# Moving three weight and operand splits at the end of a latent attention and in the routing of its mixture of experts

## The chip, the cores and the metric

The kernel runs on one core of a Trainium2 chip. The metric is the device time of the whole program in microseconds (us), as the median of several runs. The engines are named as in the profile: PE is TensorE (PEld its weight loads), DVE is VectorE, ACT is ScalarE, POOL is GpSimd and SP is SyncE, which issues the loads.

## The reference

One perceiver layer for 256 tokens of 512 features, in float32:

```python
x = x + xattn(layernorm(x), ctx)    # 1 head of 512, 4096 context rows + the 256 tokens
x = x + mla(layernorm(x))           # 16 heads, query rank 192, key/value rank 128, rotary part 64, causal
x = x + moe(layernorm(x))           # 32 routed experts of width 256, 8 a token out of 4 of 8 groups, and a shared expert
# mla: out = concat_h(softmax(q_h k_h^T * scale) v_h) @ Wo
# moe: sum_e weight_e * (silu(x Wg_e) * (x Wu_e)) @ Wd_e + shared(x)
```

The kernel computes every expert for every token and multiplies by the routing weight, which is zero for the experts not chosen. The shared expert is stored as experts 0 and 1 of 34, with weight 1.

## The kernel before

**Precision.** Each float32 operand is used as a pair: a high part, rounded by a cast, and a low part, the difference. A product is three matmuls, high by high, high by low and low by high (`product`, lines 411 to 415). So every weight and every intermediate result needs a cast on ACT (`split_hi`, line 277; `out_hi`, 305) and then a subtraction on DVE (`split_lo`, 282; `out_lo`, 309).

**Weights** come in tiles through a ring of two slots (`Tile`, `slot = s % 2`), each in two loads by SP (line 369), part a with piece 0 and part b with pieces 1 and 2. A load waits until the low part of the piece that was in its slot is made (`lo_split`). `split_hi` waits for its load and until PE has used the piece before (`used`); `split_lo` waits for `split_hi`; PE waits for `split_lo` (`ready`). A tile of the attention (`T_M + pair`) has piece 0, the projections of two heads (896 columns), and piece 1, their rows of the output weights Wo (1024). A tile of an expert (`T_E + e`) has piece 0 (gate weights and a quarter of up, 1280), piece 1 (down, 1024) and piece 2 (the rest of up, 768).

**Order.** Every engine's instructions are written out by hand and run in that order; the engines meet in counting semaphores. `ev_lo` counts the low parts of results that DVE has made, and PE waits for values of it.

**The latent attention** handles its 16 heads as 8 pairs. In `pair_step(j, s)` PE scores pair s, projects pair s + 1, transposes the softmax of pair s and multiplies the output of pair s - 1 by its rows of Wo. ACT and DVE handle the results; at the end of the step ACT makes the high parts of piece 0 of tile s + 3 and of Wo of pair s + 1, and DVE the low part of piece 0 of tile s + 3. The low part of Wo of pair s DVE makes at the beginning of step s. Steps 5 and 6, the last in the loop, split the first pieces of experts 0 and 1, which stand in the ring behind the attention. The low part of the last Wo tile (pair 7, `Tile(0, T_M + PAIRS - 1)`, piece 1) is made by POOL, behind its rotary work and ahead of two small roots for the norm.

**The tail** handles pair 7 on its own, by halves of the queries: PE runs `values_pair` of pair 6, `score_last`, then the Wo product of pair 6 behind the low part of its output (`pair_out_lo`). DVE masks the scores (`last_bias`), ACT exponentiates (`last_exp`), DVE normalizes, PE transposes (line 830), and so on to the residual, the third norm (`norm_stats`, `normalize`) and the transposed tokens (`xt_hi`, `xt_lo`). Then `expert_rows` runs experts 0 and 1 by half of the tokens, in the order (0, half 0), (1, half 0), with the second half's transposes in the middle, (0, half 1), (1, half 1).

**The experts.** PE alternates `gate_up` of one expert and `down` of the expert before: expert 2, down 1, expert 3, down 2, expert 4, down 3, and so on. DVE makes the hidden rows (`expert_product`, line 1555) and, after ACT's cast (line 1175), their low part (`expert_lo`, 1560), then the splits of later weights (`expert_splits(j, s)`: piece 1 of expert s + 1 and pieces 0 and 2 of expert s + 2 of the step), then adds the expert's rows to the residual (`expert_add`, 1548). The routing (lines 1574 to 1620, some 30 small DVE instructions) runs between expert 0's add and expert 1's. In it stand `expert_product(1, 0)` and `expert_lo(1, 0)`, which are of expert 2.

Of the kernel before, what the change touches and what calls it, by code (L numbers as in the profile page):

```python
# [45 lines left out]
PAIRS = HEADS // 2  # L46
# [12 lines left out]
T_WQ, T_WK, T_CT, T_WV, T_CN, T_WO, T_QKV, T_M = 0, 1, 2, 10, 11, 19, 20, 21  # L59
T_E = T_M + PAIRS  # L60
# [6 lines left out]
M_SIZES = (896, 1024)  # L67
E_SIZES = (1280, 1024, 768)
# [42 lines left out]
def perceiver_layer(nc, x, small, wq, wk, wv, wo, ctx_t, ctx_n, w_qkv, w_rope, w_mla, w_exp, out):  # L111
    with ExitStack() as ctx:
# [3 lines left out]
        def sem(name):  # L116
            return ctx.enter_context(nc.semaphore(name))
# [109 lines left out]
        lo_split = [sem(f"lo_split{k}") for k in range(3)]  # L227
# [44 lines left out]
        def split_hi(act, t, k, sizes, first=False):  # L272
            act.wait_ge((loaded_b if k else loaded_a)[t.slot], t.loaded)
            if not first:
                act.wait_ge(used[k], t.free(k))
            at, n = OFF[k], sizes[k]
            act.copy(w_hi[:, t.slot, at:at + n], raw[:, t.slot, at:at + n]).then_inc(hi_split[k], 1)  # L277

        def split_lo(eng, t, k, sizes):
            eng.wait_ge(hi_split[k], t.split(k))  # L280
            at, n = OFF[k], sizes[k]
            eng.tensor_tensor(w_lo[:, t.slot, at:at + n], raw[:, t.slot, at:at + n],  # L282
                              w_hi[:, t.slot, at:at + n].bitcast(F32), ALU.subtract) \
               .then_inc(lo_split[k], 1)
# [690 lines left out]
        def _(act):  # L975
# [97 lines left out]
            def pair_qk_hi(j, s, hd):  # L1073
                out_hi(act, 4 + 3 * hd, j * 2 + ((F7 if hd else F4)["qk"] + s), flat(mqk_hi[:, hd, :, :]), 512)
# [4 lines left out]
            def pair_out_hi(j, s):  # L1079
                out_hi(act, 5, j * 2 + (F5["o"] + s), flat(mo_hi[:, :, :]), 512)  # L1080

            def head_exps(j, s, hd):
                for i, (h, at, n) in enumerate(((1, 0, T), (0, T, P))):
                    act.wait_ge(m_bias_ready, j * 8 + (4 * s + 2 * hd + i + 1))
                    k = 2 * hd + h
                    p = pair_probs[:, hd, at:at + n]
                    act.activation(p, p, ACT.Exp, bias=m_bias[:, k:k + 1], scale=-1.0,
                                   accum_out=m_sum[:, k:k + 1]).then_inc(m_exp, 1)
# [4 lines left out]
            def pair_step(j, s, sizes=M_SIZES):  # L1093
                head_exps(j, s, 0)
                if not (isinstance(j, int) and s == 0):
                    pair_out_hi(j, s - 1)
                head_exps(j, s, 1)
                for hd in range(2):
                    pair_qk_hi(j, s + 1, hd)
                    head_probs_hi(j, s, hd)  # L1100
                pair_v_hi(j, s + 1)
                split_hi(act, Tile(j, T_M + s + 3), 0, sizes)
                split_hi(act, Tile(j, T_M + s + 1), 1, M_SIZES)

            for hd in range(2):
# [7 lines left out]
                pair_step(j, 1)  # L1113
                pair_step(j, 2)
            pair_step(0, PAIRS - 3, E_SIZES)
            pair_step(0, PAIRS - 2, E_SIZES)

            def last_exp(h, hd):
                act.wait_ge(m_bias_ready, 4 * (PAIRS - 1) + 2 * h + hd + 1)
# [6 lines left out]
            def last_probs_hi(h):  # L1126
                out_hi(act, 2 + h, F23["pt"] + 2 * (PAIRS - 1), last_pt_hi[h], 256 * (h + 1))
# [7 lines left out]
            last_exp(1, 1)  # L1135
            half_hi(act, 4, F4["o_last"], mo_hi, 0, 2)
            last_probs_hi(1)
            split_hi(act, Tile(0, T_E + 1), 2, E_SIZES, first=True)
            half_hi(act, 5, F5["o_last"], mo_hi, 1, 2)
            split_hi(act, Tile(0, T_E), 1, E_SIZES)  # L1140
# [48 lines left out]
        def _(dve):  # L1189
# [8 lines left out]
            def norm_stats(h, midway=None):  # L1198

                then(dve.bn_stats(stat[:, h, :], res[:, h, :]))  # L1200
                if midway is not None:
                    midway()
                then(dve.bn_aggr(mean_var[:, h, :], stat[:, h, :]))
                dve.tensor_scalar(var_eps[:, h:h + 1], mean_var[:, h, 1:2], LN_EPS, None, ALU.add) \
                   .then_inc(var_ready, 1)

            def normalize(h, roots):

                dve.wait_ge(rstd_ready, roots)
                dve.tensor_scalar(xn[:, h, :], res[:, h, :], mean_var[:, h, 0:1], rstd[:, h:h + 1],  # L1210
                                  ALU.subtract, ALU.mult).then_inc(xn_ready, 1)
# [222 lines left out]
            def pair_step(j, s, sizes=M_SIZES):  # L1434
                n = j * (2 * PER_PAIR) + (V_MLA + s * PER_PAIR - 1)
                for hd in range(2):
                    head_bias(j, s, hd)
                split_lo(dve, Tile(j, T_M + s), 1, M_SIZES)
                head_normalize(j, s, 0)
                if not (isinstance(j, int) and s == 0):  # L1440
                    pair_out_lo(n)
                head_normalize(j, s, 1)
                for hd in range(2):
                    head_qk_lo(n + 1 + 2 * hd, hd)
                    head_probs_lo(n + 2 + 2 * hd, hd)
                pair_v_lo(n + 5, s + 1)
                split_lo(dve, Tile(j, T_M + s + 3), 0, sizes)

            for hd in range(2):
                head_qk_lo(V_M0 + hd, hd)  # L1450
# [5 lines left out]
                split_lo(dve, Tile(0, T_M + k), 0, M_SIZES)  # L1456
            for i in range(PAIRS - 3):
                pair_step(0, i)
            for i in range(PAIRS - 3, PAIRS - 1):
                pair_step(0, i, sizes=E_SIZES)  # L1460


            def last_bias(h):
# [33 lines left out]
            add_to_residual(0, F01["y"], 1, 4)  # L1497
            tokens_lo(dve, 2, V_LN3, xt_hi, xt_lo, 0)
            norm_stats(1)
            normalize(1, 8)  # L1500
            split_lo(dve, Tile(0, T_E + 1), 2, E_SIZES)
            tokens_lo(dve, 0, V_LN3 + 2, xt_hi, xt_lo, 1)
            dve.wait_ge(lo_split[1], Tile(0, T_M + PAIRS - 1).split(1))
            split_lo(dve, Tile(0, T_E), 1, E_SIZES)


# [34 lines left out]
            def expert_add(j, s):  # L1541
                for h in range(2):
                    b = 4 + 2 * (s % 2) + h
                    first = {4: F4, 5: F5, 6: F6, 7: F7}[b]["moe"]
                    dve.wait_ge(bank_full[b], j + (first + s // 2))
                    dve.wait_ge(res_done, j * 4 + (3 + 2 * s + h))
                    w = weights[:, h, bass.ds(j * 2 + s, 1)]
                    dve.scalar_tensor_tensor(out=res[:, h, :], in0=bank[b][:, :], scalar=w, in1=res[:, h, :],  # L1548
                                             op0=ALU.mult, op1=ALU.add).then_inc(res_done, 1)
# [8 lines left out]
            def expert_lo(j, s):  # L1558
                dve.wait_ge(ev_hi, j * 2 + (V_H + s))
                dve.tensor_tensor(h_lo[:, s % 2, :], h_row[:, s % 2, :], h_hi[:, s % 2, :].bitcast(F32),  # L1560
                                  ALU.subtract).then_inc(ev_lo, 1)
# [35 lines left out]
            then(dve.tensor_tensor(cubed(ties), other, own, ALU.is_equal))  # L1597
            then(dve.tensor_tensor(ties, ties, smalls[:, C_TIE:C_TIE + 128], ALU.mult))
            then(dve.tensor_tensor(beats, beats, ties, ALU.add))
            expert_lo(1, 0)  # L1600
            then(dve.tensor_reduce(rank, beats.rearrange("p (g k) -> p g k", k=GROUPS), AX, ALU.add))
            then(dve.tensor_scalar(chosen_g, rank, float(TOP_GROUPS), None, ALU.is_lt))

# [17 lines left out]
            def expert_splits(j, s):  # L1621
                split_lo(dve, Tile(j, T_E + s + 1), 1, E_SIZES)
                for k in (0, 2):
                    split_lo(dve, Tile(j, T_E + s + 2), k, E_SIZES)
# [9 lines left out]
                                             in1=res[:, h, at:at + n], op0=ALU.mult, op1=ALU.add).then_inc(res_done, 1)  # L1634

            expert_add(0, 1)
            expert_splits(1, 0)
            expert_add(1, 0)
            expert_hidden(1, 1)
# [16 lines left out]
        @block.gpsimd  # L1656
        def _(pool):
            def root(n, at, cols):

                pool.wait_ge(var_ready, n)  # L1660
                pool.tensor_tensor(rstd[:, at:at + cols], var_eps[:, at:at + cols], power[:, at:at + cols],
                                   ALU.pow).then_inc(rstd_ready, 1)

            pool.memset(zero_r.bitcast(F32)[:, :], 0.0).then_inc(zeroed, 1)
            pool.memset(power[:, :], -0.5).then_inc(power_set, 1)
            pool.wait_ge(power_set, 1)
            for h in range(2):
                root(h + 1, h, 1)
            for n, at, cols in ((3, 0, 1), (4, 1, 1), (5, 2, 2), (6, 4, 2)):
                root(n, at, cols)  # L1670
            pool.wait_ge(q_raw_ready, 4)
            for pair in range(1, PAIRS):
                if pair == 1:
                    pool.wait_ge(bank_full[5], F5["rope_t"])
                else:
                    pool.wait_ge(bank_full[3], F23["pt"] + 2 * (pair - 2))
                turn_queries(pool, pair, 3 * pair)
            pool.wait_ge(lo_split[1], Tile(0, T_M + PAIRS - 1).split(1) - 1)
            split_lo(pool, Tile(0, T_M + PAIRS - 1), 1, M_SIZES)
            for h in range(2):  # L1680
                root(7 + h, h, 1)

# [88 lines left out]
```

## Time and profile before

| what | value |
|---|---|
| median of 3 runs | 547.72 us (545.03 to 547.96) |
| profiled execution | 546.07 us, of which the span of the instructions 544.3 us |
| mean granted clock of PE | 0.987 |
| busy PE, DVE, ACT, POOL | 97%, 72%, 55%, 5% of the span |
| DMA | 85.98 MB, 158 GB/s on the mean |
| chain that ended last | PE 89%, DVE 5%, DMA 2%, ACT 2% |

"Busy" is the share of the span in which an engine has an instruction under way. PE's clock is granted at one of two levels, 2.4 GHz (1.00 in the rows) and 1.2 GHz (0.50). The chain is followed back from the last instruction through whatever released each step. Times of rows are microseconds from the first instruction.

### The profile page before, as it was taken

The page shows a single profiled execution, that of the slowest core. Times are in us where ns is not written, and L with a number is a line of the kernel's source. Part 1 is how long each engine was busy: PE and PEld are TensorE (multiplying, and loading weights), DVE is VectorE, ACT ScalarE, POOL GpSimd, SP SyncE. Part 2 cuts the span into 40 slices and gives each one's busy share as a digit, 9 for nine tenths or more (in the row PEclk, how much of TensorE's full clock was granted, in tenths as well). Part 3 has the DMA queues.
Part 4 walks back from the last instruction along what each step waited for, and adds up shares of the span by engine and source line. Part 5 has one row for each costly group of instructions (what it writes and reads, how often), then busy time and mean ns, then how long its engine had stood idle before and what let it go on. Part 6 is the DMA issues. An engine that isn't in the chain of part 4 may idle for free.

```text
span 544.3 us, 9657 instructions
## 1 busy us (share of the span) xinstructions
PE 526.4 (97%) x3454; PEld 473.8 (87%) x3454; DVE 390.8 (72%) x621; ACT 302.0 (55%) x470; POOL 25.0 (5%) x43
## 2 busy tenths in 40 slices
PE   9999999999869999989989999999999999999998
PEld 7988888887659898869879999999999999999997
DVE  6776666557696888676777677776777767777675
ACT  4664597654355676654645646456464564645632
POOL 1000000000131213020000000000000000000000
PEclk9999999999996999989999999999999999999999
DMA  8766524555022224333526554646546465564521
GB/s 289 261 222 198 188 78 155 164 173 173 8 90 83 74 81 152 116 117 101 214 92 193 212 183 164 225 142 211 182 165 223 145 210 182 165 224 145 209 69 39
DMA packets 19459, 85.98 MB, mean 158 GB/s; under 512 B 2160, under 2 KB 2416, under 8 KB 19440
## 3 DMA queue, kind: packets, MB, share of 16 engines
q1 hardware_dynamic: 19440, 85.73, 46.9%
q8 instruction: 11, 0.18, 0.1%
q14 instruction: 8, 0.07, 0.0%
HBM read 85.20 MB, written 0.52 MB: 158 GB/s over the span
## 4 chain that ended last, share of the span: by engine, by line
PE 89%; DVE 5%; DMA 2%; ACT 2%; issue 1%; SPq 0%; POOL 0%; ACTq 0%; DVEq 0%; POOLq 0%
PE bank L411 27%; PE bank L415 27%; PE bank L414 27%; DMA raw<-w_exp_dram 2%; DVE w_lo L282 2%; PE bank L483 1%; PE bank L419 1%; PE bank L555 1%; PE bank L693 1%; PE bank L420 1%; PE bank L421 1%; DVE operands L309 1%; DVE scores L1403 1%; ACT w_hi L277 1%; PE bank L713 1%
## 5 line engine op out<-in xcount | busy, mean ns | idle before, releaser
L277 ACT CAST w_hi<-raw 128x768 fp32r<-128x768 f32 (+3 forms) x158 | 159.0, 1039 | 140.2 <-PE bank L411 124.3
L282 DVE TENSOR_TENSOR w_lo<-raw,w_hi 128x1024 fp32r<-128x1024 f32 (+3 forms) x157 | 184.3, 1215 | 15.5 <-ACT w_hi L277 13.4
L411 PE MATMUL bank<-xt_hi,w_hi 128*128 128x256 f32 x544 | 154.2, 283 | 2.8 <-DVE w_lo L282 2.7
L414 PE MATMUL bank<-xt_lo,w_hi 128*128 128x256 f32 x544 | 154.0, 283 | 0.0
L415 PE MATMUL bank<-xt_hi,w_lo 128*128 128x256 f32 x544 | 154.0, 283 | 0.0
L411 PE MATMUL bank<-w_hi,operands 128*128 128x512 f32 (+1 forms) x322 | 126.4, 393 | 2.5 <-DVE operands L309 1.6
L415 PE MATMUL bank<-w_hi,operands 128*128 128x512 f32 (+1 forms) x322 | 124.6, 387 | 0.0
L414 PE MATMUL bank<-w_lo,operands 128*128 128x512 f32 (+1 forms) x322 | 124.3, 386 | 0.0
L411 PEld LDWEIGHTS bank<-xt_hi,w_hi 128*128 128x128 f32 x544 | 103.5, 190 | 4.9 <-DVE w_lo L282 3.1
L414 PEld LDWEIGHTS bank<-xt_lo,w_hi 128*128 128x128 f32 x544 | 103.5, 190 | 1.2
L415 PEld LDWEIGHTS bank<-xt_hi,w_lo 128*128 128x128 f32 x544 | 103.5, 190 | 0.0
L411 PEld LDWEIGHTS bank<-w_hi,operands 128*128 128x128 f32 x322 | 60.8, 189 | 13.1 <-DVE operands L309 1.9
L415 PEld LDWEIGHTS bank<-w_hi,operands 128*128 128x128 f32 x322 | 60.8, 189 | 12.3
L414 PEld LDWEIGHTS bank<-w_lo,operands 128*128 128x128 f32 x322 | 60.8, 189 | 10.3
L1548 DVE SCALAR_TENSOR_TENSOR first_rows<-bank,weights,first_rows 128x512 f32<-128x512 f32 x66 | 49.2, 751 | 27.2 <-PE bank L415 27.2
L309 DVE TENSOR_TENSOR operands<-bank,operands 128x512 fp32r<-128x512 f32 (+1 forms) x73 | 46.5, 675 | 26.4 <-ACT operands L305 25.5
L305 ACT ACTIVATE operands<-bank 128x512 fp32r<-128x512 f32 (+1 forms) x73 | 40.1, 586 | 30.9 <-PE bank L555 13.6
L1560 DVE TENSOR_TENSOR operands<-scores,operands 128x512 fp32r<-128x512 f32 x32 | 22.1, 692 | 43.1 <-ACT operands L1175 43.1
L1555 DVE TENSOR_TENSOR scores<-bank,scores 128x512 f32<-128x512 f32 x32 | 21.8, 682 | 1.8 <-PE bank L415 1.8
L1175 ACT CAST operands<-scores 128x512 fp32r<-128x512 f32 x32 | 19.6, 613 | 3.5 <-DVE scores L1555 3.4
L1255 DVE TENSOR_REDUCE row_max<-scores x16 | 10.8, 682 | 12.1 <-ACT scores L1004 12.1
L1169 ACT ACTIVATE scores<-bank 128x512 f32<-128x512 f32 x32 | 19.0, 594 | 0.8 <-PE bank L415 0.7
(173 smaller groups left out, 526.1 us busy)
## 6 DMA issues: line engine op xcount, KB each, us to landing
raw<-w_exp_dram SPq DMA_DIRECT2D x34, 896.0 KB, 4.6
raw<-w_exp_dram SPq DMA_DIRECT2D x34, 640.0 KB, 5.5
raw<-ctx_t_dram SPq DMA_DIRECT2D x16, 512.0 KB, 4.4
raw<-ctx_n_dram SPq DMA_DIRECT2D x16, 512.0 KB, 4.3
raw<-w_mla_dram SPq DMA_DIRECT2D x8, 512.0 KB, 3.6
raw<-w_mla_dram SPq DMA_DIRECT2D x8, 448.0 KB, 4.0
raw<-wq_dram SPq DMA_DIRECT2D x4, 256.0 KB, 5.1
raw<-wk_dram SPq DMA_DIRECT2D x2, 512.0 KB, 7.1
```

Source lines behind the costliest of these rows:

```text
L277: act.copy(w_hi[:, t.slot, at:at + n], raw[:, t.slot, at:at + n]).then_inc(hi_split[k], 1)
L282: eng.tensor_tensor(w_lo[:, t.slot, at:at + n], raw[:, t.slot, at:at + n], w_hi[:, t.slot, at:at + n].bitcast(F32), ALU.subtract) \
L305: act.activation(hi, bank[b][rows, at:at + n], ACT.Copy, scale=scale).then_inc(ev_hi, 1)
L309: dve.tensor_tensor(lo, bank[b][rows, at:at + n], hi.bitcast(F32), ALU.subtract) \
L411: ins = pe.matmul(o, a[0], b[0], start=start, stop=False)
L414: pe.matmul(o, a[0], b[1], start=False, stop=False)
L415: return pe.matmul(o, a[1], b[0], start=False, stop=stop)
L1169: act.activation(gate_act[:, s % 2, :], bank[2 * (s % 2)][:, :], ACT.Silu).then_inc(silu_ready, 1)
L1175: act.copy(h_hi[:, s % 2, :], h_row[:, s % 2, :]).then_inc(ev_hi, 1)
L1548: dve.scalar_tensor_tensor(out=res[:, h, :], in0=bank[b][:, :], scalar=w, in1=res[:, h, :], op0=ALU.mult, op1=ALU.add).then_inc(res_done, 1)
L1555: dve.tensor_tensor(h_row[:, s % 2, :], bank[up][:, :], gate_act[:, s % 2, :], ALU.mult) \
L1560: dve.tensor_tensor(h_lo[:, s % 2, :], h_row[:, s % 2, :], h_hi[:, s % 2, :].bitcast(F32), ALU.subtract).then_inc(ev_lo, 1)
```

## The change

On ACT, the cast of expert 1's piece 0 leaves step 6 of the attention and stands in the tail, behind `last_probs_hi(1)`. On DVE, its low part leaves step 6 too and stands between the second half's `norm_stats` and `normalize`. The low part of the last Wo tile moves from POOL to DVE, directly behind step 6; with it go POOL's waits for its high part and its turn and DVE's later wait for the low part. In the routing, `expert_lo(1, 0)`, expert 2's low part, moves from the middle of the routing to behind `expert_add(0, 1)`.

```diff
@@ ACT, pair_step
-                split_hi(act, Tile(j, T_M + s + 3), 0, sizes)
+                if sizes is not None:
+                    split_hi(act, Tile(j, T_M + s + 3), 0, sizes)
                 split_hi(act, Tile(j, T_M + s + 1), 1, M_SIZES)
@@ ACT, behind the loop
             pair_step(0, PAIRS - 3, E_SIZES)
-            pair_step(0, PAIRS - 2, E_SIZES)
+            pair_step(0, PAIRS - 2, None)
@@ ACT, tail
             last_probs_hi(1)
+            split_hi(act, Tile(0, T_E + 1), 0, E_SIZES)
             split_hi(act, Tile(0, T_E + 1), 2, E_SIZES, first=True)
@@ DVE, pair_step
-                split_lo(dve, Tile(j, T_M + s + 3), 0, sizes)
+                if sizes is not None:
+                    split_lo(dve, Tile(j, T_M + s + 3), 0, sizes)
@@ DVE, behind the loop
-            for i in range(PAIRS - 3, PAIRS - 1):
-                pair_step(0, i, sizes=E_SIZES)
+            pair_step(0, PAIRS - 3, sizes=E_SIZES)
+            pair_step(0, PAIRS - 2, sizes=None)
+            split_lo(dve, Tile(0, T_M + PAIRS - 1), 1, M_SIZES)
@@ DVE, tail
             norm_stats(1)
+            split_lo(dve, Tile(0, T_E + 1), 0, E_SIZES)
             normalize(1, 8)
             split_lo(dve, Tile(0, T_E + 1), 2, E_SIZES)
             tokens_lo(dve, 0, V_LN3 + 2, xt_hi, xt_lo, 1)
-            dve.wait_ge(lo_split[1], Tile(0, T_M + PAIRS - 1).split(1))
             split_lo(dve, Tile(0, T_E), 1, E_SIZES)
@@ DVE, routing
             then(dve.tensor_tensor(beats, beats, ties, ALU.add))
-            expert_lo(1, 0)
@@ DVE, behind the routing
             expert_add(0, 1)
+            expert_lo(1, 0)
             expert_splits(1, 0)
@@ POOL
-            pool.wait_ge(lo_split[1], Tile(0, T_M + PAIRS - 1).split(1) - 1)
-            split_lo(pool, Tile(0, T_M + PAIRS - 1), 1, M_SIZES)
             for h in range(2):
                 root(7 + h, h, 1)
```

## Rows read from the trace of the kernel before

**Rows 1.** The page's first part: busy us (share of the span) and instructions.
```profile
PE 526.4 (97%) x3454; PEld 473.8 (87%) x3454; DVE 390.8 (72%) x621; ACT 302.0 (55%) x470; POOL 25.0 (5%) x43
```

**Rows 2.** Windows: length, busy us (instructions) by engine, PE's granted clock, DMA.
```profile
234.00:237.40 3.40, 3.40 (x12) 2.41 (x11) 1.89 (x10) 2.50 (x9) 0.82 (x1) 0.50 0.46 112
246.14:280.78 34.64, 34.64 (x254) 32.39 (x254) 24.25 (x58) 17.71 (x24) 0.56 (x1) 1.00 0.37 137
283.44:544.30 260.86, 258.13 (x1818) 242.88 (x1818) 188.64 (x216) 137.39 (x163) 0.00 (x0) 1.00 0.52 174
```

**Rows 3.** Timeline of PE: start, us, engine, line, operation [idle before, releaser].
```profile
227.11 0.39 PE L415 MATMUL bank<-w_hi,operands 128*128 128x512 f32 x1
...
228.56 0.27 PE L415 MATMUL bank<-operands 128*128 128x128 f32 x1
...
230.55 0.62 PE L817 MATMUL bank<-operands 64*128 64x256 f32 x6
...
233.28 0.51 PE L411 MATMUL bank<-w_hi,operands 128*128 128x512 f32 x1 [1.56 <-DVE operands L309]
...
235.46 0.63 PE L830 MATMUL bank<-first_rows,scores 128*128 128x128 f32 x2
...
243.14 0.50 PE L411 MATMUL bank<-w_hi,operands 128*128 128x512 f32 x1 [0.93 <-DVE operands L330]
...
246.14 0.35 PE L411 MATMUL bank<-w_hi,xt_hi 128*128 128x256 f32 x1 [0.90 <-DVE xt_lo L330]
...
277.87 0.39 PE L411 MATMUL bank<-w_hi,operands 128*128 128x512 f32 x1
...
283.44 0.39 PE L411 MATMUL bank<-xt_hi,w_hi 128*128 128x256 f32 x1 [2.66 <-DVE w_lo L282]
```

**Rows 4.** The chain that ended last, from 223 to 232 us: start, us, what.
```profile
223.13 6.65 DMA raw<-w_exp_dram
229.80 1.27 ACT w_hi L277
231.09 1.49 DVE w_lo L282
```

**Rows 5.** Timeline of DVE in and behind the routing.
```profile
275.26 0.69 DVE L1560 TENSOR_TENSOR operands<-scores,operands 128x512 fp32r<-128x512 f32 x1 [2.82 <-ACT operands L1175]
275.87 0.28 DVE L1601 TENSOR_REDUCE scores<-scores 128x16 f32<-128x128 f32 x1
...
279.44 1.41 DVE L1548 SCALAR_TENSOR_TENSOR first_rows<-bank,weights,first_rows 128x512 f32<-128x512 f32 x2
280.77 3.49 DVE L282 TENSOR_TENSOR w_lo<-raw,w_hi 128x1024 fp32r<-128x1024 f32 x3
```

**Rows 6.** Timeline of ACT beside the routing.
```profile
272.43 2.21 ACT L277 CAST w_hi<-raw 128x1024 fp32r<-128x1024 f32 x2 [4.79 <-PE bank L411]
274.55 0.61 ACT L1175 CAST operands<-scores 128x512 fp32r<-128x512 f32 x1
```

**Rows 7.** Timeline of DVE in the tail of the latent attention.
```profile
224.55 3.08 DVE L309 TENSOR_TENSOR operands<-bank,operands 128x512 fp32r<-128x512 f32 x5
...
233.14 0.34 DVE L1403 CUSTOM_DVE_ANT_0 scores<-bank,smalls,q_neg 128x128 f32<-128x128 f32 x1
...
248.01 0.55 DVE L1210 TENSOR_SCALAR xn<-first_rows,mean_var,rstd 128x512 f32<-128x512 f32 x1 [0.68 <-POOL rstd L1661]
...
251.35 0.76 DVE L330 TENSOR_TENSOR xt_lo<-bank,xt_hi 128x256 fp32r<-128x256 f32 x2 [1.93 <-ACT xt_hi L325]
252.02 1.22 DVE L282 TENSOR_TENSOR w_lo<-raw,w_hi 128x1024 fp32r<-128x1024 f32 x1
```

**Rows 8.** Timeline of POOL in the tail.
```profile
232.15 2.67 POOL L282 TENSOR_TENSOR w_lo<-raw,w_hi 128x1024 fp32r<-128x1024 f32 x1 [14.45 <-ACT w_hi L277]
```

**Rows 9.** Timeline of ACT in the tail.
```profile
242.24 0.38 ACT L325 ACTIVATE operands<-bank 128x256 fp32r<-128x256 f32 x1 [1.65 <-PE bank L415]
```

**Rows 10.** Window of PE alone in the first step of the latent attention.
```profile
162.30:172.50 10.20, 8.94 (x49) 0.50 0.21 67
```

## The prediction

> **What bounds the kernel now.** I read the page first: PE is busy for 97% of the span, so time can only leave where PE waits or runs at the lower of its clock's two levels [rows 1]. I then cut the span into stretches at PE's gaps [rows 2]. The last 261 us, the experts' loop, are PE-bound (258.13 us busy of 260.86), and so are 246.14 to 280.78, without an idle moment. Two places are not: 231.72 to 246.14, the tail of the attention, and the stretch of 2.66 us before 283.44 in which PE does nothing while DVE works through all of it.
>
> PE's own rows give the sizes [rows 3]: gaps of 1.56 us before 233.28, 0.93 before 243.14, 0.90 before 246.14 and 2.66 before 283.44. The chain of waits says what stood before the first [rows 4]: the 640 KB piece of expert 1's weights (`Tile(0, T_E + 1)`, piece 0) is on its way for 6.65 us and lands at 229.8, ACT casts it, DVE makes its low part until 232.58, and only behind that come the two halves of `pair_out`, for which PE asks at 231.72. Nobody needs that weight before 249. The gap of 2.66 us is DVE's queue too [rows 5]: in `expert_lo(1, 0)` DVE waits 2.82 us for ACT's cast of expert 2's hidden rows, which stands behind two weight casts that could begin only when PE began expert 3 [rows 6]. Routing, the adds and the weight splits are queued behind that wait, and PE waits for the low part of expert 4's piece 0.
>
> **Part A, the weight out of the loop's last step, the low part of Wo 7 on DVE.** ACT loses a cast of 1.27 us [rows 4] and the wait for its DMA. It can take Wo 7's cast when PE has freed the slot, at about 227.5 [rows 3], and is done at 228.6 (1.1 us, half of the pair in [rows 6]). `pair_out_hi` follows the end of `values_pair` (228.83) and ends near 229.5 (0.6 us, a cast of 512 columns in [rows 6]). DVE's last operand ends at 227.6 [rows 7], so the split of Wo 7 goes 228.6 to 229.8, priced at 1.22 us by the same shape in [rows 7], against 2.67 us on POOL [rows 8], and `pair_out_lo` (0.69 us, as a low part of 512 columns in [rows 5]) ends at 230.5. PE asks at 231.72, so DVE's added 1.22 us lies under PE's scores with 1.2 us to spare, and the gap of 1.56 us is gone. If that cover were gone, each us beyond it would be PE's.
>
> What is late next is the last pair's softmax. DVE began its masked scores at 233.14 [rows 7] and can now do so when bank 2 is full, 231.17: 1.97 us earlier. From there the tail is a chain over DVE, ACT and PE (scores, exponents, transposes, values, last output half, residual, norm) up to the first expert product at 246.14. So the whole chain moves by 1.97 us, not 1.56; bounds are 1.56 and 1.97 and I take 1.95, since DVE and not PE is waited for in the two later gaps. Those (0.93 and 0.90) stay, and small gaps of 0.2 to 0.3 us open ahead of transposes and values.
>
> The clock: from 234.0 to 237.4 the granted clock was 0.50, the 1.2 GHz level, after PE had stood for 1.56 us [rows 2, 3]. Without the gap I expect the full clock. That halves 3.4 us of PE time (1.7 us), but little of it is on the chain: two transposes took 0.63 us [rows 3] and would take half, and the values behind them had to wait for a slow half output product. I take 0.5 us; bounds 0 (the clock falls anyway) and 1.7.
>
> **Part B, piece 0 of expert 1 in the tail.** ACT's cast, 1.27 us, now stands after `last_probs_hi(1)`, ahead of piece 2's cast and of `half_hi(5)`. ACT is idle for 1.65 us there [rows 9]: 0.4 us to spare, cost nothing. DVE's 1.49 us stand between `norm_stats(1)` and `normalize(1, 8)`. DVE idles 0.68 us (for POOL's root) and 1.93 us behind it [rows 7], 2.6 us together. The second half's `xn` is done 0.8 us later, near 249.3 in the old times, while PE transposes it at 250.5. PE now needs the piece 24 products of 0.12 us after 246.14, at 249.02, and the low part ends at 247.32 + 1.49 = 248.81: 0.2 us to spare. Cost nothing; at worst the whole 1.49 us, at best nothing gained.
>
> The queues: SP's next loads (expert 1's pieces 1 and 2, then expert 2's piece 0) wait for Wo 7's low part, now 229.8 instead of 234.8, so they come earlier. The load into the slot's piece 0 for expert 3 now waits for a low part at 248.8 instead of 232.6, but in SP's queue it stands behind a load that waits for DVE's split at 252.02 [rows 7], so nothing changes. POOL loses its wait and its split; only the two small roots are queued behind them.
>
> **Part C, expert 2's low part later.** Without the wait DVE goes from 272.43 straight on. From 275.87 to 279.44, 3.57 us of routing, then `expert_add(0, 1)` 1.33 us [rows 5]: the add ends at 277.33. `expert_lo(1, 0)` takes 0.69 us, until 278.04. PE wants it at 277.87 [rows 3], so a new gap of about 0.25 us opens there. Then come expert 3's piece 1 and expert 4's piece 0, 2304 of the 3072 columns that take 3.49 us, so 2.6 us, until 280.6. PE, 0.25 us late, ends expert 2's down at 280.85 and finds the piece. It starts expert 4 at about 280.9 instead of 283.44: 2.5 us gained. Nothing later gives it back: ACT had its casts at 274.6 [rows 6], and in the loop DVE is busy for 188.64 of 260.86 us [rows 2]. Bounds: 1.2 us (DVE's chain from 272.43 longer by 1.3) and 2.8.
>
> **The sum.** The profiled execution took 546.07 us, 544.3 of span and 1.8 around it. 546.07 - 1.95 - 0.5 - 2.5 = 541.1. That execution is 1.65 us under the median of the three runs (547.72); from the median the same sum gives 542.8. Which base applies hangs on the clock. In this execution the gap of 2.66 us was not followed by the lower level (clock 1.00 from 283.44 on), while one of 1.56 us was. So in another run the longer gap may well be; a stretch like that of 3.4 us costs up to 1.7 us in the PE-bound experts, which is the distance to the median. I take a value between the two, a little nearer to the first, since its rows are the ones I can see: **541.8**.
>
> The rule I weighed stands in the Trainium skill, TensorE: Matmul & The Clock Gate, Part 1: the gate follows how busy PE has been, and where it acts differs between runs of one kernel. By it the run at the median may have lost its 1.7 us behind a gap that this change closes, and the result would be the 541.1 of the first sum. The trace agrees only in part: two like gaps, one drop.
>
> **The rivals.**
> (1) Only the routing gap closes, or only the tail. If the tail's time comes back (the piece's split makes PE wait at 249, the softmax chain isn't shortened), 2.5 us remain: 546.9, the mean of both bases, less 2.5 is 544.4. If the tail gains and the routing doesn't (ACT is late by the same amount elsewhere), 2.45 us remain: 544.5. For it: margins of 0.2 us in B and a new wait in C. Against: a missed margin costs its excess, not the whole. 12%.
> (2) The clock falls at another place. The tail keeps two gaps of 0.9 us, with 1.4 us of work between them. One stretch of 3.4 us at half clock behind them lies on the experts' rows, where PE is the bound: 541.8 + 1.7 = 543.5. For it: before, the drop fell on work that others held up, so it cost little there. Against: behind the same two gaps the clock stayed at 1.00 in the trace. 17%. The rule of the Trainium skill named above allows this one too; no row here tells how often.
> (3) The other side. Between 162.3 and 172.5 the clock was at half for 10.2 us, though PE was busy for 8.94 of them [rows 10]. If the two tail gaps bring such a stretch onto the experts' rows, it costs 5.1 us, and the 0.5 us is not won: 546.9 - 1.95 - 2.5 + 5.1 = 547.6, slower than 546.9. It decides from a stretch of 9 us on. For it: the gaps move together with the rest, no farther apart. Against: the same gaps in the trace were not followed by a drop. 4%.
> (4) It doesn't do what it says: the wait of 231.72 is in truth one for the values of the pair before. Against it: `values_pair` ended at 228.83, and the chain of waits leads from DVE's split to the matmul at 233.28. 541.8 + 2.45 = 544.3; 3%.
>
> **How the numbers follow.** Forecast 64%: 541.8, its own range 540.0 to 543.2. The lowest run less the whole sum is 545.03 - 4.95 = 540.1; I go to 539.8 below, since 0.3 us of the clock term's upper bound may come too. Above, rivals 1 and 2 reach 544.5; I stop at 544.8. About 0.5% (2.7 us) is what a measurement of this kernel can tell from no change, so faster means below 545.0. The forecast, rival 2 and half of 1 and 4, which lie 0.6 us under that bound, are faster: 0.88, less something for the spread of 2.9 us among the runs: 0.82. Same 0.15, slower 0.03.
>
> **What would show it.** A: no gap of PE near 231.7, masked scores near 231.2, clock 1.00 from 234 to 237.4, first expert product near 243.7. B: DVE's 128x1280 split between the norm's statistics and `xn`, no PE gap before the 25th product. C: DVE goes through the routing without a wait, PE starts expert 4 some 34.8 us after its first expert product, where it was 37.3. It is wrong if the tail's gaps grow by as much as the first one shrinks, if PE waits over 0.5 us for expert 2's low part, or if a half-clock stretch appears after 244.

## The result and the profile after

The changed kernel takes 541.48 us at the median (539.39 to 544.02, 8 runs), the kernel before in the same comparison 546.56 us (544.70 to 548.70, 8 runs). The ratio is 0.991, with a 95% interval of 0.988 to 0.994: 0.9% faster. The forecast was 541.8.

The profiled execution of the changed kernel is the longest of its eight, 544.02 us with a span of 542.2 us. The page's busy times, against [rows 1]:

```profile
PE 527.2 (97%) x3454; PEld 474.6 (88%) x3454; DVE 391.9 (72%) x622; ACT 302.2 (56%) x470; POOL 23.5 (4%) x42
```

POOL has one instruction fewer and DVE one more: the low part of the last output weights. The timeline of PE answers [rows 3]:

```profile
228.82 0.28 PE L411 MATMUL bank<-operands 128*128 128x256 f32 x1
...
232.01 0.62 PE L817 MATMUL bank<-operands 64*128 64x256 f32 x6
...
233.03 0.39 PE L411 MATMUL bank<-w_hi,operands 128*128 128x512 f32 x1
...
234.78 0.44 PE L830 MATMUL bank<-first_rows,scores 128*128 128x128 f32 x2 [0.20 <-DVE scores L1481]
...
236.15 0.33 PE L411 MATMUL bank<-operands 128*128 128x128 f32 x1 [0.24 <-DVE operands L309]
...
242.12 0.71 PE L411 MATMUL bank<-w_hi,operands 128*128 128x512 f32 x1 [0.93 <-DVE operands L330]
...
246.49 0.35 PE L411 MATMUL bank<-w_hi,xt_hi 128*128 128x256 f32 x1 [0.69 <-DVE xt_lo L330]
...
278.64 0.49 PE L411 MATMUL bank<-w_hi,operands 128*128 128x512 f32 x1 [0.26 <-DVE operands L1564]
...
281.50 0.28 PE L411 MATMUL bank<-xt_hi,w_hi 128*128 128x256 f32 x1
```

The product at 233.03 follows the scores without a gap, where 1.56 us stood. Expert 2's down product at 278.64 waits 0.26 us, and expert 4 at 281.50 does not wait, where 2.66 us stood. DVE now makes the low part of the last output weights in a pause, and its next work waits for PE's scores, not PE for DVE:

```profile
230.16 1.23 DVE L282 TENSOR_TENSOR w_lo<-raw,w_hi 128x1024 fp32r<-128x1024 f32 x1 [1.07 <-ACT w_hi L277]
...
232.68 0.35 DVE L1405 CUSTOM_DVE_ANT_0 scores<-bank,smalls,q_neg 128x128 f32<-128x128 f32 x1 [0.70 <-PE bank L817]
```

DVE's queue answers [rows 5]: two instructions of the routing that the old wait stood between, and at the end expert 1's add, the moved low part and the splits:

```profile
272.49 0.29 DVE L1603 TENSOR_TENSOR scores<-scores 128x128 f32<-128x128 f32 x1
272.82 0.29 DVE L1604 TENSOR_REDUCE scores<-scores 128x16 f32<-128x128 f32 x1
...
276.41 1.41 DVE L1552 SCALAR_TENSOR_TENSOR first_rows<-bank,weights,first_rows 128x512 f32<-128x512 f32 x2
277.73 0.68 DVE L1564 TENSOR_TENSOR operands<-scores,operands 128x512 fp32r<-128x512 f32 x1
278.33 3.49 DVE L282 TENSOR_TENSOR w_lo<-raw,w_hi 128x1024 fp32r<-128x1024 f32 x3
```

What this execution lost again is in the clock. Two windows of it, with the columns of [rows 2] (length, busy us of PE, PEld, DVE, ACT and POOL, PE's granted clock, DMA's share and GB/s):

```profile
234.00:237.40 3.40, 2.96 (x17) 1.97 (x16) 1.89 (x9) 2.38 (x7) 0.00 (x0) 1.00 0.93 352
242.55:245.95 3.40, 3.25 (x10) 2.22 (x8) 0.87 (x3) 0.49 (x2) 0.00 (x0) 0.54 0.00 0
```

The stretch at the 1.2 GHz level is gone from 234 and now begins at 242.2, behind the gap of 0.93 us that ends at 242.12. From the start of `values_pair` to the last half of the output product, 15.80 us became 13.30. From there to the first expert product, 3.00 us became 4.37.

**How times are compared below.** Executions of one kernel differ by up to 6 us, and nearly all of that is this clock. In the profiles where it falls, it stays low for 3.4, 6.8 or 10.2 us at a time, and each 3.4 us at half clock (a stretch, below) lower the granted clock over the span by 0.003. Sorted by the granted clock of the execution, the mean times in us (number of runs) are:

| kernel | 0.997 | 0.994 | 0.991 | 0.987 | 0.984 |
|---|---|---|---|---|---|
| before (67) | | 544.4 (9) | 545.5 (18) | 547.1 (27) | 548.5 (11) |
| changed (20) | 539.2 (3) | 540.6 (5) | 541.5 (5) | 543.2 (6) | 545.1 (1) |

Two more runs of before were lower still. A fit over all runs, with a base for each kernel and one price for a stretch of 3.4 us, gives 1.31 us for a stretch and bases known to 0.2 us. A base is thus an estimate of the time without any stretch; it takes a stretch to cost the same wherever it falls, which is true only on the mean. Each experiment below is told by its median, its ratio, this base and its mean number of stretches. The kernel before has base 541.8 and 3.7 stretches, the changed one (both of its sets of runs) 537.9 and 2.85. So of some 4.9 us of gain between the means (546.6 and 541.6), 3.9 us stand at equal clock and 1.1 us are the clock's.

### The profile page after: what moved, and what is told of

Its sections match the earlier page's. It is cut to its first block, busy times and chain, and to the rows that moved or that the text cites. A ratio compares the mean times of both kernels' runs of the same rounds, so it can differ in the third digit from the quotient of the medians.

```text
span 542.2 us, 9654 instructions
## 1 busy us (share of the span) xinstructions
PE 527.2 (97%) x3454; PEld 474.6 (88%) x3454; DVE 391.9 (72%) x622; ACT 302.2 (56%) x470; POOL 23.5 (4%) x42
## 4 chain that ended last, share of the span: by engine, by line
PE 90%; DVE 5%; ACT 2%; DMA 1%; issue 1%; SPq 0%; DVEq 0%; ACTq 0%
PE bank L411 27%; PE bank L415 27%; PE bank L414 27%; PE bank L419 2%; PE bank L420 1%; PE bank L421 1%; DMA raw<-wq_dram 1%; DVE w_lo L282 1%; PE bank L555 1%; PE bank L693 1%; PE bank L713 1%; DVE operands L309 1%; PE bank L674 1%; DVE scores L1405 1%; PE bank L437 0%
## 5 line engine op out<-in xcount | busy, mean ns | idle before, releaser
L282 DVE TENSOR_TENSOR w_lo<-raw,w_hi 128x768 fp32r<-128x768 f32 (+3 forms) x158 | 185.4, 1215 | 13.2 <-ACT w_hi L277 10.9
```

## The experiments

### The tail alone

The changed kernel with expert 2's low part back in the routing:

```diff
             then(dve.tensor_tensor(beats, beats, ties, ALU.add))
+            expert_lo(1, 0)
...
             expert_add(0, 1)
-            expert_lo(1, 0)
```

> Parts A and B of the change alone; expert 2's low part stays in the middle of the routing, as before. My theory (the two parts gain apart and their gains add): PE's gap ahead of expert 4, 2.66 us before, is still there with 2.5 to 2.8 us; the time is 2.5 us (2.0 to 3.2) above the changed kernel's 541.5, so near 544.0, and 1.5 to 3.0 us below the kernel before. The stretch from the start of pair 6's value products to the last half of the last output product is 13.3 us long, as after the change, against 15.8 before. Rival (the routing gap only existed because the tail was late): the gap is below 1 us here too and the time is within 1 us of the changed kernel's. Second rival (the clock falls behind the long gap in most executions): the time is up to 1.7 us higher still, 545.7, and this execution shows a granted clock of 0.50 behind the gap.

545.28 us (541.89 to 547.37, 12 runs), ratio 0.998 (0.996 to 1.001) to the kernel before: in the measured times nothing that can be told from no change. The base is 540.3, 1.5 us below before, but with 3.8 stretches. PE's timeline and two windows (length, busy PE, granted clock, DMA):

```profile
240.35 0.50 PE L411 MATMUL bank<-w_hi,operands 128*128 128x512 f32 x1 [0.93 <-DVE operands L330]
243.33 0.36 PE L411 MATMUL bank<-w_hi,xt_hi 128*128 128x256 f32 x1 [0.90 <-DVE xt_lo L330]
...
280.65 0.58 PE L411 MATMUL bank<-xt_hi,w_hi 128*128 128x256 f32 x1 [2.66 <-DVE w_lo L282]
```
```profile
280.30:283.70 3.40, 3.05 (x14) 0.50 0.97 300
283.70:300.00 16.30, 16.30 (x116) 1.00 0.57 194
```

The gap of 2.66 us is untouched by the earlier tail, so the first rival falls. Behind it PE works at half clock for 3.4 us, which the profiled execution of before did not show, and the time is as high as the second rival said. `values_pair` to the first expert product takes 16.28 us here (227.05 to 243.33).

### The routing alone

The kernel before with only this edit:

```diff
             then(dve.tensor_tensor(beats, beats, ties, ALU.add))
-            expert_lo(1, 0)
...
             expert_add(0, 1)
+            expert_lo(1, 0)
```

> Part C alone: expert 2's low part moves behind expert 1's add, the tail is as before. My theory: PE has a gap of 0.2 to 0.3 us ahead of expert 2's down product and none ahead of expert 4; the gap of 1.56 us in the tail stays; the time is 2.5 us (2.2 to 4) below the kernel before. Together with the gain of the other half it makes the whole 5.1 us within 1 us. Rival (a gap filled early is waited for again later): PE shows a new gap of over 1 us somewhere in the experts' loop and the gain is under 1.5 us.

542.24 us (541.22 to 543.86, 12 runs), ratio 0.993 (0.991 to 0.995), 3.9 us below before. The base is 539.4, 2.4 us lower, as forecast for the gap. The other 1.7 us or so are 2.3 stretches instead of 3.7. The gap behind the scores is smaller here than in [rows 3]; PE, and the DMA in the chain of waits:

```profile
233.41 0.50 PE L411 MATMUL bank<-w_hi,operands 128*128 128x512 f32 x1 [1.07 <-DVE operands L309]
...
245.68 0.36 PE L411 MATMUL bank<-w_hi,xt_hi 128*128 128x256 f32 x1 [0.90 <-DVE xt_lo L330]
...
277.83 0.50 PE L411 MATMUL bank<-w_hi,operands 128*128 128x512 f32 x1 [0.24 <-DVE operands L1560]
```
```profile
223.74 6.17 DMA raw<-w_exp_dram
229.93 1.27 ACT w_hi L277
```

The load's start and PE's scores are both 0.6 us later here than in [rows 4] and [rows 3], so that alone changes nothing. But the piece took 6.17 us to land and not 6.65, and these 0.48 us are the difference between the two gaps. The gap hangs on how long a load takes, and 1.56 us was a long case of it. The tail takes 17.72 us (`values_pair` at 227.96), with no stretch in it. Against 16.28 us in the kernel above, the tail's gain at full clock is 1.44 us.

The two halves gain 1.2 us and 4.1 us on the mean of their runs (545.3 and 542.4 against 546.6), the whole change 4.9. In the bases they add exactly (1.5 and 2.4 of 3.9 us). In the means they add within the scatter, and the share of each depends on the order: beside the other half already in place, the tail is worth 0.8 us and the routing 3.7.

### The last output weights on POOL again

```diff
@@ DVE
-            split_lo(dve, Tile(0, T_M + PAIRS - 1), 1, M_SIZES)
...
+            dve.wait_ge(lo_split[1], Tile(0, T_M + PAIRS - 1).split(1))
             split_lo(dve, Tile(0, T_E), 1, E_SIZES)
@@ POOL
+            pool.wait_ge(lo_split[1], Tile(0, T_M + PAIRS - 1).split(1) - 1)
+            split_lo(pool, Tile(0, T_M + PAIRS - 1), 1, M_SIZES)
```

> The changed kernel with the low part of the last output weights made by POOL again (2.67 us there against 1.22 on DVE), and the later wait for it back on DVE. My theory (what paid in part A was the removal of expert 1's piece from DVE's queue, not the engine of the last low part): time within 0.5 us of the changed kernel's, the wait of PE near 231.7 does not come back, the masked scores begin right behind bank 2. Rival (the engine matters: POOL's 2.67 us end too late, or slow DVE while both run): PE waits for the last output weights or the masked scores take longer than 0.34 and 0.48 us, and the time is 0.5 to 1.5 us higher.

540.29 us (539.89 to 541.25, 6 runs), ratio 0.990 (0.986 to 0.993). The base, 537.6, is within 0.3 us of the changed kernel's, and the tail takes 16.29 us. So the runs show no difference between the two engines for this low part. The timeline of POOL shows why it could stay:

```profile
227.47 2.38 POOL L282 TENSOR_TENSOR w_lo<-raw,w_hi 128x1024 fp32r<-128x1024 f32 x1 [11.07 <-ACT w_hi L277]
```

It starts 4.7 us earlier than in [rows 8] since ACT's cast is no longer behind the other one. The lower median comes from 2.2 stretches; six runs do not say that this is more than chance.

### The piece of expert 1 back in the loop

```diff
-            pair_step(0, PAIRS - 2, None)
+            pair_step(0, PAIRS - 2, E_SIZES)
...
-            split_hi(act, Tile(0, T_E + 1), 0, E_SIZES)
...
-            pair_step(0, PAIRS - 2, sizes=None)
+            pair_step(0, PAIRS - 2, sizes=E_SIZES)
...
-            split_lo(dve, Tile(0, T_E + 1), 0, E_SIZES)
```

> The changed kernel with both splits of expert 1's piece 0 back in step 6 of the latent attention, so that on DVE the last output weights' low part (1.22 us) stands behind it. My theory (the removal of the piece is the whole gain of part A, and DVE's new 1.22 us are free only without it): PE's gap behind the last scores is 1.56 + 1.2 = 2.7 us, and the time is 3 to 4 us above the changed kernel's, so 544.5 to 545.5: above what part C alone gives by about 1.2 us. Rival (the DMA of that piece was not what held ACT up; the split only filled a pause): the gap is under 1 us and the time within 1 us of the changed kernel's.

545.09 us (542.51 to 545.77, 12 runs), ratio 0.997 (0.995 to 0.999); base 540.1, 3.6 stretches. DVE's two splits and PE's gap:

```profile
230.19 2.63 DVE L282 TENSOR_TENSOR w_lo<-raw,w_hi 128x1280 fp32r<-128x1280 f32 x2 [3.27 <-ACT w_hi L277]
```
```profile
233.47 0.79 PE L411 MATMUL bank<-w_hi,operands 128*128 128x512 f32 x1 [2.46 <-DVE operands L309]
```

The gap was expected at 2.7 us. The base is 0.7 us over that of the routing alone and 2.2 over the changed kernel's. With the kernel above it settles part A: the piece in step 6 is the cause of the gap, and DVE's new 1.22 us are free only once the piece is out. ACT's cast and DVE's low part went back together, so no run tells their shares apart.

### The changed kernel again

> The changed kernel once more, beside the three others of this call. With 1.36 us for each stretch of 3.4 us at half clock (a fit over all executions so far of time against granted clock, with a base of its own for each kernel) it has a base of 537.8 us. Theory: the median is 541.0 to 542.0 and the executions lie on that line within 0.5 us. Rival (the lower median of the kernel with POOL's low part, 540.3, is a gain of its own): the changed kernel has at equal granted clock 0.5 us or more above 540.3.

541.48 us (538.98 to 545.13, 12 runs), ratio 0.991 (0.989 to 0.994): the same median. In this profile the tail has no stretch at half clock; `values_pair` (226.95) to the first expert product (243.23) takes 16.28 us.

### Zeros in the routing gap

The tail alone, with PE kept busy while it waits; the loop's first pass is written out:

```diff
+            gate_up(1, 1, told=used[1])
+            down(1, 0, told=used[2])
+            for _ in range(10):
+                zeros(0, True)
+            gate_up(1, 2, told=used[1])
+            down(1, 1, told=used[2])
-            with pe.Fori(1, NE // 2 - 1) as j:
+            with pe.Fori(2, NE // 2 - 1) as j:
```

> Parts A and B alone, with the routing gap left, and in it ten matmuls of zeros (512 columns each, some 2.3 us) between expert 2's down product and expert 4. They compute nothing that is used. Theory (part C gains 2.5 us by the gap itself and another 1.4 to 1.7 us because the lower clock level often follows the gap): PE still waits for expert 4's low part, 0.3 to 0.5 us behind the zeros, expert 4 begins as late as without them, but the granted clock stays at 1.00 there; the mean number of half-clock stretches falls from 3.8 to 2.8 or less, and the median is 1.0 to 2.0 us below the 545.3 of the same kernel without the zeros, near 543.7. Rival (the clock has no part in the gap's cost): the time stays at 545.3 within 0.5 us.

543.31 us (541.11 to 545.81, 10 runs), ratio 0.994 (0.991 to 0.997), with 2.4 stretches instead of 3.8 and 2.0 us below the same kernel without the zeros. PE, then a window behind the gap:

```profile
276.62 2.43 PE L483 MATMUL bank<-zero_r 128*128 128x512 f32 x10
279.44 0.39 PE L411 MATMUL bank<-xt_hi,w_hi 128*128 128x256 f32 x1 [0.39 <-DVE w_lo L282]
```
```profile
279.40:283.00 3.60, 3.56 (x29) 1.00 0.82 298
```

Expert 4 is as late as it was (37.31 us behind the first expert product, 37.32 without the zeros), and the time falls by 2.0 us nevertheless. The 1.4 stretches fewer account for 1.9 us by the price above. This is the share of the routing gap's cost that was the clock's. The loop's first pass is written out here too, which no run tried by itself; the bases, 539.9 and 540.3, leave little for it.

### Zeros in the tail's two gaps

```diff
+            for _ in range(3):
+                zeros(7, True)
             pe.wait_ge(ev_lo, n + 3)
             out_pair(last, last=True, halves=(1,))
...
             transpose_half(xn, 0, 2, xn_ready, 5, told=used[1])
+            for _ in range(3):
+                zeros(7, True)
```

> The changed kernel with three matmuls of zeros (0.7 us) in each of the two gaps of 0.9 us that the tail keeps, ahead of the last half of the output product and ahead of the first expert product. Theory (the tail gained less than its gaps say since the clock falls behind the two remaining gaps in part of the executions, as in the profiled one of the changed kernel, and there costs 1.4 us): no half-clock stretch near 242, the mean number of stretches 0.3 to 0.6 lower than the changed kernel's 2.9, the median 0.5 to 1.0 us below it. Rival (the zeros only push the work behind them): the same number of stretches and a time up to 0.5 us higher.

541.47 us (540.36 to 542.08, 6 runs), ratio 0.991 (0.987 to 0.994); base 538.0, 2.5 stretches. The difference to the changed kernel, 0.0 us at the median and 0.35 at the mean, is within the scatter. The expected 0.5 to 1.0 us did not show. It decides nothing; it shows only that the zeros cost nothing at equal clock.

### The piece split twice

```diff
+            dve.wait_ge(hi_split[0], Tile(0, T_E + 1).split(0))
+            then(dve.tensor_tensor(w_lo[...], raw[...], w_hi[...], ALU.subtract))
             split_lo(dve, Tile(0, T_E + 1), 0, E_SIZES)
             normalize(1, 8)
```

> The changed kernel with the low part of expert 1's piece 0 made twice in the tail, so that DVE's 1.49 us there become 3.0. Theory (part B is free only within a slack of 0.2 to 0.3 us): PE has a new gap of 1.1 to 1.3 us ahead of the first product of expert 1's rows, and the time is 1.2 us higher than the changed kernel's (0.8 to 2.8, since the gap may bring a stretch at half clock). Rival (DVE has 1.5 us and more to spare there): no such gap, time within 0.5 us.

543.01 us (539.92 to 544.69, 10 runs), ratio 0.993 (0.990 to 0.996), 1.5 us above the changed kernel at the median; base 538.5, 0.65 us above it. In the profile PE was at half clock from 240.6 to 247.5, so that it came late itself and shows no gap ahead of expert 1's rows. Another execution of it:

> One more look at the changed kernel with expert 1's piece 0 split twice on DVE: its first profile had PE at half clock in this very place, which hid the wait. Theory (the slack of part B is 0.3 us at full clock): if the clock is full between 243 and 248, PE has a gap of 1.1 to 1.3 us ahead of the first product of expert 1's rows. Rival: no gap at full clock either.

544.60 us, and again PE was at half clock there, from 242 to 249. So the cost of the doubled split lies between 0.65 us (equal clock) and 1.5 us (medians), which says that the slack is well under 1.49 us. At the granted clocks 0.997 and 0.994 alone its four runs lie 0.8 us above the changed kernel's eight, while at 0.984 (four runs against one) nothing is lost, as it would be where PE is slow itself. The gap of 1.1 to 1.3 us was not seen, since the slow clock hid it both times. The changed kernel's rows give a slack of 0.3 us: in its repeated run the low part is made at 245.82, and PE comes to its 25th expert product at

```profile
246.17 0.28 PE L411 MATMUL bank<-w_hi,xt_hi 128*128 128x256 f32 x1
```

No run confirms that size.

### Zeros at the start of the latent attention

```diff
+            def fill(j, s, first, second):
+                for _ in range((first, second)[s] if isinstance(j, int) and s < 2 else 0):
+                    zeros(0, True)
...
+                fill(j, s, 4, 8)
                 pe.wait_ge(ev_lo, n - 1 if start else n - 2)
                 rope_scores(told=used[0] if start else None)
...
+                fill(j, s, 4, 0)
                 transpose_head(0, normed, rope, told=used[0])
```

> The changed kernel with matmuls of zeros in three gaps of PE at the start of the latent attention (four ahead of step 0's scores, four ahead of step 0's transposes, eight ahead of step 1's scores). In all profiles so far two or three stretches at half clock begin near 162 to 165, behind these gaps of 1.0, 1.1 and 1.9 us. Theory (the clock follows PE's idle time, whatever the reason, and costs 1.3 us for a stretch): the stretch of 7 to 10 us there is gone, the mean number of half-clock stretches falls from 2.9 to 1 or less, and the median lies 2 to 3.5 us below the changed kernel's 541.5, near 539. Rival (the stretch is set by something else, such as the kinds of matmul there): it stays, and the time is 541.5 to 542.5.

537.68 us (537.31 to 538.74, 6 runs), ratio to before 0.983 (0.980 to 0.986), 3.8 us below the changed kernel; base 537.6, 0.2 stretches. The longest fill and a window behind it, against [rows 10]:

```profile
161.98 2.09 PE L483 MATMUL bank<-zero_r 128*128 128x512 f32 x8
```
```profile
163.90:173.00 9.10, 9.00 (x77) 1.00 0.28 92
```

The low clock is gone here, and with it more than was expected: the mean fell from 2.85 stretches to 0.2. The eleven profiles without these zeros have two or three stretches in this place, 2.4 in the mean, so it held most of them; six runs do not say whether those elsewhere are rarer too. The base is the same as the changed kernel's within 0.4 us, so the gain is the clock's alone.

### Zeros in five gaps, and the low part ahead of the add

```diff
+            expert_lo(1, 0)
             expert_add(0, 1)
-            expert_lo(1, 0)
```

> The kernel with zeros at the start of the latent attention, and beside that zeros in the tail's two gaps and expert 2's low part ahead of expert 1's add instead of behind it. Theory: the gap of 0.25 us ahead of expert 2's down product is gone (0.25 us less), and the tail's stretches at half clock too, so the median is 0.3 to 1.0 us below that of the kernel with zeros at the start alone. Rival (the add is late now and holds up the splits): a gap of 0.2 us or more ahead of expert 4.

537.33 us (537.07 to 537.69, 6 runs), ratio 0.982 (0.979 to 0.985): on the mean 9.2 us less than the kernel before at 546.6, and the fastest here. No PE gap is left in the routing, ahead of expert 2's down product or ahead of expert 4, so its rival falls. Its granted clock was 1.00 in every run, and the runs lie within 0.6 us of each other. It is 0.35 us below the kernel above at the median and 0.2 us in the base; the closed gap of 0.26 us is the likely cause, but the zeros in the tail came in with it and the two were not told apart.

## Why the prediction was right, and where it was not

**Part A, the gap.** Right: it is gone, and the masked scores follow bank 2 at once (232.68 in the changed kernel, 0.05 us behind the scores' end). `pair_out_lo` ends at 231.98 and PE asks for it at 233.19: 1.2 us to spare, as forecast. From `values_pair` to the last output half the two profiled executions differ by 2.50 us, where 1.95 + 0.5 was forecast. As the gain of the typical execution the sum is too large: at full clock the tail went from 17.72 to 16.28 us, 1.44 us, and the bases say 1.5. The step that failed is the lower bound of 1.56. I took the one gap of one execution as the rule, and with it the 1.97 us of the chain. It hangs on when a load lands, 1.07 us in the second profile. That the chain moves by more than the gap was right: 0.37 us more there (1.44 against 1.07), where 0.41 us were forecast.

**Part A, the clock.** Wrong. "Without the gap I expect the full clock" held at 234 and not for the tail: the changed kernel's profiled execution has its stretch 8 us later, from 242.2 to 245.6, where the tail waits for PE, at 1.37 us. That it reaches behind 244 is one of the prediction's own signs of being wrong. This was rival 2, in some executions and not in most: of the eleven profiles whose tail keeps both gaps of 0.9 us three show the clock falling behind the first of them. The price of 0.5 us for the stretch at 234 fits the rows: the tail took 18.80 us with it (227.34 to 246.14) and 17.72 without it and with 0.49 us less of gap, which leaves 0.6 us. What failed is that it would be gone: the tail alone has 3.8 stretches in the mean against 3.7, so the 0.5 us was not there on the mean.

**Part B.** Right as far as the profiles show: no wait of PE for the piece in any kernel that has it in the tail, except as told above for the doubled one. Its own last step was not quite right. `normalize(1, 8)` did not start when DVE's split was done but 0.46 us later, for a reason told in the last section. It cost nothing, as PE came to the transposes of that result only at 250.9.

**Part C.** Right in each step: a new gap of 0.26 us (0.25 forecast), none ahead of expert 4, DVE through the routing without a pause. From the first expert product to expert 4 it takes 35.01 us (34.8 forecast, 37.30 before). The size at equal clock, 2.4 us, was forecast as 2.5.

**The base.** The sum ran to 541.1 from the profiled execution, and I took 541.8 because the long gap "may well be" followed by the lower clock in other runs. The tail alone shows that stretch, and the zeros in the gap take 2.0 us off with expert 4 as late as before. The routing alone has 1.4 stretches fewer than before. So part C was worth 3.7 to 4.1 us and not 2.5, part A and B 0.8 to 1.2 and not 2.45, and the total came out right (4.9 for 4.95) since the two errors nearly cancel. That is luck. The base behind the 541.8, some 546.75, was right too: 67 runs of the kernel before have a mean of 546.6.

## What to carry to other kernels

A gap of the engine that sets the pace has two prices: its length, and a stretch at the lower clock behind it in some of the executions. Read several executions' granted clocks beside their times before pricing a gap from one, and price a gap that ends on a load with more than one profile. Where a gap can't be closed, matmuls that nobody reads kept the clock up here and cost nothing: three fills were worth 3.8 us, against 4.9 us for closing two gaps.

## What the runs showed of the hardware

**A stretch at half clock costs 1.31 us (plus or minus 0.04) where it lasts 3.4 us**, over 167 runs of eleven kernels. That is less than the 1.7 us of PE time lost in it, probably since some of it lies beside waits, as the one at 234 does, which cost 0.6 us.

**How often the clock fell behind a gap differs from gap to gap.** At the start of the latent attention PE waits 1.95 us in every profile without zeros there. In the kernel before:

```profile
163.56 1.54 PE L693 MATMUL bank<-operands 64*128 64x256 f32 x12 [1.95 <-DVE operands L309]
```

In all eleven such profiles the clock falls to the 1.2 GHz level in this gap or up to 1.8 us behind it, for 6.8 or 10.2 us; in the two with zeros it does not. Behind the first gap of 0.93 us in the tail it fell in three of eleven, at the gap of 2.66 us ahead of expert 4 in one of two, and behind that of 1.07 us of the routing alone it did not.

**POOL's tiny root waits for DVE's split.** The root for the second half's norm takes 0.56 us on POOL in the kernel before and 1.74 us in every kernel that has expert 1's piece in the tail. POOL and DVE in the repeated run of the changed kernel:

```profile
239.69 0.56 POOL L1665 TENSOR_TENSOR rstd<-var_eps,power 128x1 f32<-128x1 f32 x1 [22.45 <-DVE var_eps L1206]
244.50 1.74 POOL L1665 TENSOR_TENSOR rstd<-var_eps,power 128x1 f32<-128x1 f32 x1 [4.26 <-DVE var_eps L1206]
```
```profile
244.34 1.48 DVE L282 TENSOR_TENSOR w_lo<-raw,w_hi 128x1280 fp32r<-128x1280 f32 x1
246.28 0.55 DVE L1212 TENSOR_SCALAR xn<-first_rows,mean_var,rstd 128x512 f32<-128x512 f32 x1 [0.45 <-POOL rstd L1665]
```

The root starts 0.16 us into the split and ends 0.42 us behind its end, for one column; `xn` waits for it. With the piece split twice it again takes 1.74 us and ends 0.42 us behind the first of the two splits. The Trainium skill, GPSIMD Engine Reference, section 8, says that POOL shares its SBUF interfaces with VectorE and contends with VectorE instructions that have two SBUF inputs, which the split has. The trace agrees: with DVE's split elsewhere the root took 0.55 to 0.56 us. I had placed the root under the split at no cost.
